# One vision-transformer layer with a delta-rule attention: the solve of a head pair moved beside the next pair's substitution, with scores in two PSUM homes

## What is computed

```python
q = _causal_dw_conv_silu(x @ Wq, conv_q)      # 4 taps in time
k = _causal_dw_conv_silu(x @ Wk, conv_k)
v = _causal_dw_conv_silu(x @ Wv, conv_v)
q, k = _l2norm(q), _l2norm(k)
def step(state, inp):
    q_t, k_t, v_t, a_t, b_t = inp
    retained = jnp.einsum('bhvk,bhk->bhv', state, k_t)
    state = a4 * (state - b4 * rk) + b4 * vk   # rk, vk: outer products with k_t
    o_t = jnp.einsum('bhvk,bhk->bhv', state, q_t)
    return (state, o_t)
out = out * rms * o_norm_w * jax.nn.silu(x @ Wg)
return out @ Wo
```

## Time and profile before

| | |
|---|---|
| median of 3 runs | 259.45 us (259.29 to 260.57) |
| the profiled execution | 259.83 us |
| its span in the trace | 257.7 us |
| PE busy | 196.8 us (76%) |
| DVE busy | 155.4 us (60%) |
| ACT busy | 80.9 us (31%) |
| POOL busy | 65.9 us (26%) |

### The profile page before, as it was taken

One profiled execution on the slowest core, in us unless ns is written; L12 is line 12 of the kernel. 1 busy time (PEld: TensorE's weight loads), 2 busy tenths in 40 slices (PEclk: granted clock), 3 DMA queues, 4 the chain that ended last, 5 costly groups with the idle time before them and its releaser, 6 DMA issues.

```text
span 257.7 us, 5506 instructions
## 1 busy us (share of the span) xinstructions
PE 196.8 (76%) x2304; PEld 148.6 (58%) x2304; DVE 155.4 (60%) x340; ACT 80.9 (31%) x156; POOL 65.9 (26%) x70
## 2 busy tenths in 40 slices
PE   8999867896799959079998743799790699998050
PEld 4776546364587836067885422599550599896030
DVE  0215887998966653986659098935709824022864
ACT  2009974033652334035430533320022020030632
POOL 7000016400002540800164053003606200062732
PEclk9999999559599998757999795559568555599855
DMA  6999000000000000000000000000000000000002
GB/s 182 301 307 340 3 0 3 0 1 4 0 3 3 3 3 0 0 1 3 3 3 3 0 0 0 0 3 6 0 3 3 0 3 3 3 0 0 0 0 94
DMA packets 7023, 8.23 MB, mean 32 GB/s; under 512 B 1439, under 2 KB 5487, under 8 KB 6999
## 3 DMA queue, kind: packets, MB, share of 16 engines
q1 hardware_dynamic: 6373, 7.78, 9.7%
q10 hardware_dynamic: 626, 0.10, 0.2%
HBM read 7.27 MB, written 0.61 MB: 31 GB/s over the span
## 4 chain that ended last, share of the span: by engine, by line
PE 52%; DVE 30%; issue 8%; ACT 5%; POOL 3%; DVEq 1%; POOLq 0%; ACTq 0%
PE PY L1126 13%; PE PA L1015 10%; DVE conv L628 9%; PE PA L1024 6%; PE PS L1110 5%; PE PS L1069 4%; DVE tri L746 4%; DVE tmp L741 3%; PE PR L1145 3%; PE PA L995 3%; PE PS L995 2%; DVE xg L687 2%; PE PR L1078 2%; DVE osum L783 2%; PE PR L1087 1%
## 5 line engine op out<-in xcount | busy, mean ns | idle before, releaser
L628 DVE SCALAR_TENSOR_TENSOR conv<-xp,tap_sb,conv 128x592 f32<-128x592 f32 x60 | 53.8, 899 | 7.8 <-ACT conv L434 6.8
L339 POOL TENSOR_TENSOR Xd<-E,cst 104x320 f32<-104x320 f32 x8 | 8.9, 1115 | 110.3 <-DVE E L680 110.3
L775 DVE TENSOR_TENSOR y<-R,PY 104x512 f32<-104x512 f32 x24 | 16.5, 686 | 27.3 <-PE PY L1126 27.3
L1126 PE MATMUL PY<-y,ZP 40*40 40x64 f32 x768 | 30.4, 247 | 0.0
L449 ACT ACTIVATE KQ<-conv 128x592 f32<-128x592 f32 x16 | 11.3, 707 | 60.5 <-DVE conv L628 60.4
L1126 PEld LDWEIGHTS PY<-y,ZP 40*40 40x40 f32 x768 | 28.2, 136 | 3.0 <-issue 2.6
L355 POOL TENSOR_TENSOR onrm<-omean,mhalf_c 104x8 f32<-104x8 f32 x8 | 14.2, 1774 | 53.4 <-DVE omean L786 53.4
L1015 PE MATMUL PA<-hT,wk_sb 128*128 128x296 f32 x64 | 23.6, 526 | 1.9 <-ACT xp L425 1.4
L425 ACT ACTIVATE xp<-PA 128x296 f32<-128x296 f32 x40 | 15.3, 414 | 26.5 <-PE PA L1015 26.5
L1135 PE MATMUL PA<-cst,ogn 104*128 104x104 f32 x32 | 5.8, 352 | 22.2 <-ACT xp L425 14.5
L1015 PEld LDWEIGHTS PA<-hT,wk_sb 128*128 128x128 f32 x64 | 14.9, 243 | 9.1 <-issue 6.9
(11 more groups left out here) (144 smaller groups left out, 328.1 us busy)
## 6 DMA issues: line engine op xcount, KB each, us to landing
x_sb<-xT SPq DMA_DIRECT2D x12, 144.0 KB, 3.4
wk_sb<-wk SPq DMA_DIRECT2D x4, 256.0 KB, 6.9
wq_sb<-wq SPq DMA_DIRECT2D x4, 256.0 KB, 7.0
wlin_sb<-wlin SPq DMA_DIRECT2D x6, 128.0 KB, 3.4
wv_sb<-wv SPq DMA_DIRECT2D x4, 128.0 KB, 6.9
wg_sb<-wg SPq DMA_DIRECT2D x4, 128.0 KB, 6.8
wo_sb<-wo SPq DMA_DIRECT2D x1, 512.0 KB, 6.7
out_rows<-res SPq DMA_DIRECT2D x1, 384.0 KB, 2.6
```

Source lines behind the costliest of these rows:

```text
L628: dve.scalar_tensor_tensor(y_c, xp[c][:, j:j + NSEQ * TP].rearrange("p (n t) -> p n t", t=TP)[:, :, 0:T], tap_sb[:, i:i + 1], y_c, ALU.mul ...
L775: dve.tensor_tensor(y[h][:, :, :], R[:, :, h, :], PY[0:ROWS, h, :].rearrange("p (n v) -> p n v", v=VD), ALU.subtract).then_inc(y_made, 1)
L1126: mm = pe.matmul(PY[r, h, n * VD:(n + 1) * VD], ZP[h][r, n, at:at + TP], y[h][r, n, :] if j else R[r, n, h, :], start=True, stop=True)
```

## The change

The loop now runs over u = -1 to 3. A turn holds the scores and the substitution of pair v = u + 1 and, beside the nine substitution steps, the solve of pair u; the normalization of the output of pair u - 1 falls into it too. The projection of the values (c = 4) moves from pair w to pair v, at the end of the turn, and with it `v_trans`, `rhs` and `silu(4, ...)` move to the next turn. Scores and `zp` of head 1 go to `PY` instead of `PS`; `E` and `kn` get a second buffer for every other pair. Output products of the first pairs stand between the rounds of the last solve. No product and no elementwise operation is added or left out.

```diff
-        E = [sb(f"E{h}", [ROWS, NCP, 2, TP]) for h in range(2)]
+        E = [[sb(f"E{p}{h}", [ROWS, NCP, 2, TP]) for h in range(2)] for p in range(2)]
+        PYN = PY[:, :, :].rearrange("p b n -> p (b n)").rearrange("p (n c) -> p n c", c=P)
+        SC = (PSN, PYN)
...
             def scores(h, v):
-                if h == 1:
-                    pe.wait_ge(e_made, 2 * v + 1)
-                elif v > 0:
-                    pe.wait_ge(zp_copied, 4 * v)
+                if h == 0 and v > 1:
+                    pe.wait_ge(zp_copied, 4 * (v - 2) + 2)
+                if h == 1 and v > 1:
+                    pe.wait_ge(osb_made, 2 * (v - 1))
...
             def solve(h, j, u):
                 if j == 0:
-                    pe.wait_ge(zp_copied, 4 * u + 2 * h + 2)
+                    pe.wait_ge(zp_copied, 4 * u + 4)
...
```

More of the change, by code:

```diff
@@ L142, in vit_layer @@
         cs = sb("cs", [ROWS, 2 * NCP])
-        kn = sb("kn", [ROWS, 2 * NCP])
+        kn = [sb(f"kn{p}", [ROWS, 2 * NCP]) for p in range(2)]
         eq = sb("eq", [ROWS, 2, 2, NCP])
@@ L803, in _ @@
             dve.wait_ge(cst_loaded, 16)
-            scan(0, 0)
-            scan(1, 0)
             taps(2, 0)
-            decayed(0, 0)
             taps(3, 0)
-            decayed(1, 0)
-            taps(4, 0)
-            block_scales(0)
-            scaled_block(0)
-            spread(0, 0)
-            spread(1, 0)
-            taps(0, 1)
-            sub_start(0)
-            rhs(0, 0)
-            rhs(1, 0)
-            for m in range(BL - 1, 0, -1):
-                sub_product(m, 0)
-                if m == 6: q_norm(0)
-                if m == 9: tap(1, 1, 1)
-                if m == 8: tap(1, 2, 1)
-                if m == 7: tap(1, 3, 1)
-                sub_difference(m, 0)
-            split_alpha()
-            sub_end(0)
-            expand(0, 0)
-            expand(1, 0)
-            taps(2, 1)
-            taps(3, 1)
             def out_weights():
@@ L1007, in _, with project @@
             w_of = ((wk_sb, wk_loaded, 0), (wq_sb, wq_loaded, 0), (wk_sb, wk_loaded, 1), (wq_sb, wq_loaded, 1), (wv_sb, wv_loaded, 0))
-            def project(c, w):
+            def project(c, w, halves=(0, 1)):
                 wt, landed, h = w_of[c]
                 pe.wait_ge(landed[w], 16)
-                for half in range(2):
-                    take(half, xp_copied, 10 * w + 2 * c + half + 1)
+                for half in halves:
+                    take(half, xp_copied[c], 2 * w + half + 1)
                     for k in range(DC):
@@ L1016, in project, with gates @@
                                        hT[:, k, half * HTOK:(half + 1) * HTOK], start=(k == 0), stop=(k == DC - 1))
-                    mm.then_inc(proj_done, 1)
-            def gates(p):
+                    mm.then_inc(proj_done[c], 1)
+            def gates(p, halves=(0, 1)):
                 pe.wait_ge(wg_loaded[p], 16)
-                for half in range(2):
+                for half in halves:
                     take(half, gate_silu, 2 * p + half + 1)
@@ L1158, in _ @@
             pe.wait_ge(alpha_act, 5)
-            spread_alpha(0, 0)
-            spread_alpha(1, 0)
-            project(4, 0)
-            scores(0, 0)
-            project(0, 1)
-            scores(1, 0)
-            project(1, 1)
-            q_norm(0, 0)
-            q_norm(1, 0)
-            v_trans(0)
-            replicate(0, 0)
-            replicate(1, 0)
-            project(2, 1)
-            project(3, 1)
-            project(4, 1)
-            pe.wait_ge(parts_step, 7)
-            for u in range(NPAIR):
+            for u in range(-1, NPAIR):
```

215 lines of the change are left out of this document (79 added, 136 removed).

## The result

The changed kernel takes 242.51 us (median of 4 runs, 239.95 to 243.39) against 259.37 us (4 runs, 258.53 to 260.57): ratio 0.933, interval 0.925 to 0.941. Six more runs later gave 239.85 us (239.71 to 243.20), ratio 0.929 (0.923 to 0.935). The forecast was 247.0 us, with a range of 228 to 259. TensorE's clock does not come back at the same place in every execution, so that the runs of one version lie 1 to 17 us apart; where this matters I give the range.

What follows compares the result with a forecast made beforehand. Bound by solve and substitution following each other, then by PE's clock. Terms 64.5 + 42.3 + 42.7 + 39.3 + 37.4 + 19.1 = 245.3 us of span; with 2.1 us outside 247.4, less 0.4 for the median 247.0 us; range 228 to 259.

Steps and rivals of the forecast that it cites:

- Ahead of the first overlapped turn: From the kernel's start to the scan of pair 1, with no solve done by then: 64.5 us.
- Turn 0: First overlapped turn, from the scan of pair 1 to that of pair 2: 42.3 us, 35.6 at the full clock.
- Wait A: Substitution on DVE waits for replicate, queued on PE behind project(2, w): 3.0 us in turn 0, 4.5 in turn 1.
- Wait B: End of turns 0 and 1, DVE waiting for PE's rounds, projections and gates: 5.7 us in turn 0, 1.3 + 1.8 in turn 1.
- Turn 1: Second overlapped turn, from the scan of pair 2 to that of pair 3: 42.7 us, 38.7 at the full clock.
- DVE floor: Shortest overlapped turn: DVE's 32.9 us of work and 1.5 us of gaps between dependent operations, 34.4 us.
- Turn 2: From the scan of pair 3 to the first tap of the last values, PE deciding at 1.2 GHz: 39.3 us.
- serial piece: End of turn 2: project(4, 3) last in PE's queue, 3.2 us, then its copy and first tap, 1.2 us.
- Turn 3: From the first tap of the last values through the last solve to the end of the output products: 37.4 us.
- the overlap: Solve rounds fitting beside DVE's substitution steps; the rival that they would not gave 258 to 260 us, chance 0.08.
- rival 1: Whole kernel: a denser PE holds 2.4 GHz throughout, 220.1 us of span, 222 us; chance 0.22 for 222 to 235 us.
- the second home: Separate buffer for scores of head 1: worth nothing, since PE never reaches those scores before ACT is ready.

Runs made afterwards that it cites:

- the exchange: Changed kernel with project(2, w) put behind the replication instead of ahead of it: 235.57 us, ratio 0.906.
- the filler at the end: Changed kernel with eleven full-width products that nobody reads ahead of the last o_trans: 239.72 us (236.74 to 243.67).
- both fillers: Unread full-width products added to the changed kernel in two separate runs: in turn 2, 244.00 us; ahead of the last o_trans, 239.72 us.

## Why the prediction was right, point by point

The sum was 245.3 us of span, the trace has 241.3.

- **Ahead of the first overlapped turn**: 64.5 us forecast, 64.4 measured.
- **Turn 0**: 42.3 forecast, 37.1 measured. Wait A was 3.5 us (3.0 forecast), with the projection at the half clock (4.29 us), as charged. Wait B was 2.8 instead of 5.7: 1.6 us at the end and 1.3 us for a round. I had taken the fall of the clock among the first four rounds as certain and for long. It came for one round and half a projection only (88.6 to 92.0 us). This term was the largest miss. The 1.6 us for scores at the half clock were nil, and DVE without its waits needed 30.8 us, 1.2 less than the floor I had set.
- **Turn 1**: 42.7 forecast, 38.9 measured. Wait A 4.8 (4.5 forecast), wait B 0.9 (3.1 forecast). The clock was 1.00 through the rounds. The wait for the scores of head 1, 0.7 us, was 0.3, and the DVE floor of 34.4 us was 1.5 us too high.
- **Turn 2**: 39.3 forecast, 40.1 measured, with the clock at half through the rounds, as charged. The 8.8 us wait for the values was the serial piece that the prediction named; moving it took 8 to 10 us off, part of it by the clock.
- **Turn 3**: 37.4 forecast, 41.7 measured. To the first round it was 8.0 (7.5). Rounds, products and gates took 19.5 us to the end of the gates (18.3): the clock came back at 197.8 us, later than I took. The step that failed is the end, 13.8 us instead of 11.1. I had credited 1.1 us for moving the products away, without asking what PE would do in their place. It idled, and the clock fell.
- **The tail**: 19.1 and 19.1 us.

So 8.9 us too many in turns 0 and 1 and 5.1 too few in turns 2 and 3 made a forecast that is 4.0 us off. Its sum is better than its terms, and that is luck. The larger part of both misses is the clock; some 2.7 us of the first are the DVE floor. The rivals: the clock did not stay up throughout (0.70 and 0.75 in turns 2 and 3), turns did not reach 47 us, and the overlap came about. For rival 1 the prediction had counted the longest idle time of PE as gone; idle stretches of 3.2 to 3.8 us stayed in every turn, each with a fall of the clock. Two slips changed nothing: the terms ahead of the first turn add up to 63.6 us and not 64.0, and those of a worst turn 1 to 46.7 us and not 49. That a measurement tells 0.5% was too much to claim: the ten runs of the changed kernel alone spread over 1.5%. That the second home is worth nothing was confirmed by its removal; that wait A comes from the queue, by the exchange.

Open are the exact conditions under which the grant returns in turn 3. The traces with a return at 187.6 and at 197.8 us have the same instructions up to there, at times that differ by less than 0.1 us.

## What to carry to other kernels

When two chains are laid beside each other, walk every queue for what now stands ahead of the short instruction that somebody waits for: exchanging two statements was worth 5 us here in two turns, and moving one projection out of the last place 8 to 10 us, part of it by the clock. Put full-width products between small ones, and ahead of them, where the clock matters. Work moved out of the end of a kernel gained nothing here, since idle time took its place.

## What the runs showed of the hardware

- Products on 40 rows do not hold 2.4 GHz even without a gap: in the kernel before the grant fell at 181 us with PE busy 2.00 of 2.00 us, and with the wide products moved away it stayed 0.50 at 2.00 of 2.00. They don't lose it at once: behind the early projection of the values six rounds and an `o_trans`, 6.8 us in all, ran at the full clock (161.45 to 168.27 us).
- Idle stretches of 2.7 to 6.3 us go with seven of the eight falls in the changed kernel's trace. With the last one in the attention filled, the grant stayed 1.00 there.
- One program can have times in two or three separate groups (239.8 and 243.2 us; 231 to 233, 238 to 242 and 248 us), because the grant returns at 187.6 us in one execution and at 205.4 us in another. The median of the same kernel moved from 232.5 us (four runs) to 239.7 us (six runs), so that a few runs can't tell 3% here.
- A 128x296 product in float32 shows as two passes. A projection of 8 passes takes 2.26 us at the full clock and 4.28 us at the half clock, 0.28 and 0.54 us a pass, and the filler at the end was 22 passes in 5.64 us, 0.26 each. Counting passes instead of products would have sized both fillers nearly rightly.
